# A four-stage kernel (attention, experts, RWKV mixing, experts): fillings over x, an earlier start of the expert stages, batch 6 placed by itself, row tables on GpSimd

## The chip, the cores and the metric

One core of one Trainium2 chip runs the whole program in one launch. The metric is the device time of one execution in microseconds. Engines are TensorE (PE), VectorE (DVE), ScalarE (ACT), GpSimd (POOL) and SyncE (SP, which only issues DMAs here).

## What is computed

x has 8 batches of 512 tokens with 256 channels, all fp32. Four blocks follow each other, each added to x:

```
x = x + attention(layernorm(x))      # linear attention, rope, 3-tap convolution
x = x + experts(layernorm(x))        # 8 experts, top 2 per token, SwiGLU, width 512
x = x + rwkv(x)                      # time mixing (scan over tokens), channel mixing
x = x + experts(layernorm(x))        # same gate and weights
```

The expert block scores 4096 tokens with a gate, takes the best two experts of each, sorts the 8192 pairs by expert and sends each group through its expert's three matrices.

## The kernel before, in words

**Stages.** `phase_attention`, `phase_experts` ("first_"), `phase_mix` (tiles "b_") and `phase_experts` ("second_") run one behind the other, each a block of five hand-written engine programs that wait for each other by semaphores. Between two blocks all engines meet; behind the attention there are two such meetings, one of them after its semaphores are cleared.

**Attention** goes over the batches with two tile sets. ACT normalises, PE transposes (`transposes`, L1066), ACT and DVE write the transposed rows as a high and a low fp32r half (`evacuate_next`, `low_part`), and PE forms every product out of three of such halves (L164 to L166). Beside it the expert matrices are loaded, split and stored: seven experts in the periods (`high_part`, `weight_low`), the eighth as an extra piece in the periods 0, 5 and 6 (`load_extra` and `store_extra` on SP, `high_extra` on ACT, `low_extra` L940 on DVE). In a period DVE runs `low_extra` ahead of the quotient `a_u` and of `a_v` (L1025), and PE's next projections into bank q2 wait for `a_v`. PE's first projection also waits for the semaphore `loaded` (the DMAs of the gate and of `vectors`, the last that SP issues behind the whole of x).

**Routing.** Each token pair needs its row in the sorted table. DVE makes one-hot tables per group of four tiles (one batch): `hot_blocks` (L320, 128x960) and `hot_rows` (L330, 128x1024). ACT scales the first by the token number (`send_tokens`, L349), PE adds up eight products per group in one bank (`place_tokens`, L440), and `order_tokens` (L450) sorts the result. Six groups are early; batches 6 and 7 are late and are ranked together (`late_choices`, `count_choices`, `late_places`, `late_hots`, `final_places`), once the last batch's top experts are known. In the attention the lane numbers that DVE compares with lie in PSUM, in mixing in SBUF.

**Handover.** DVE copies the first row numbers to `gather_token`, and POOL issues three gathers (`first_gathers`, L421) ahead of the end of the stage. In `phase_experts` PE issues 16 fillings (`keep_busy`, L194: products into a bank that nobody reads), waits for the tables that DVE makes of the block bounds (L1356 to L1370, `table_ready`), and only then transposes the first 128 gathered rows (`transpose_x`, L1424). DVE evacuates them (L1377, L1379) behind its tables. After that 71 blocks run, pipelined over two tile sets.

**Mixing.** The head is the serial part: statistics of batch 0, ACT `norm(0)` (L1629), transposes (L2139), `evacuate_xn`, `mix_time`, products k, v, r (`project`, L2158), the scans (L1962, L2006, L2008), `den`, its reciprocal (L2013), `gT` (L2016), `time_product` (L2146). POOL forms `num` for batch 0 in six instructions and then `fk_lo`, the low half of the first channel matrix (L1883); ACT makes `fk_hi` (L1777) behind `carry(0)`, after all weights are in. PE fills with `const.ones` as both operands (128 columns, 44 and 16 of them) and with `fk_hi` (512 columns, 16). Periods follow, in which batch b's channel mixing runs beside batch b+1's time mixing. `finish(b-1, 1)` (L2050) frees the fourth bank of `key_products` (L2233). POOL's `add_channel` adds the result to x.

```
def keep_busy(nc, out, stationary, moving, times):
    for _ in range(times):
        nc.tensor.matmul(out, stationary, moving, start=True, stop=True)
```

Of the kernel before, what the change touches and what calls it, by code (L numbers as in the profile page):

```python
# [44 lines left out]
class Constants:  # L45
# [6 lines left out]
    keep_late: object  # L52
    ones: object
# [170 lines left out]
class Route:  # L224


    def __init__(self, hots, ranks, small, rounded, row_hot, block_hot, sent, bank, placed, sem):
        self.hot = Shelf(hots).take([P, TOPK, EX, T])
        s = Shelf(rounded)
        self.both_early, self.both_late = s.take([P, EX, TE]), s.take([P, EX, TL])  # L230
# [4 lines left out]
        self.earlier_late, self.rank_late, self.chosen_late = s.take([P, EX, TL]), s.take([P, EX, TL]), s.take([P, TOPK, EX, TL])  # L235
# [10 lines left out]
        cells, late = EX * TE, EX * TL  # L246
        self.before, self.all = early_bank[:, 0:cells], early_bank[:, cells:2 * cells]
        self.before_late, self.all_late = late_bank[:, 0:late], late_bank[:, late:2 * late]
# [4 lines left out]
        self.block_hot_ready, self.row_hot_ready = sem("r_block_hot_ready"), sem("r_row_hot_ready")  # L253
        self.sent_ready, self.sent_used = sem("r_sent_ready"), sem("r_sent_used")
# [3 lines left out]
def early_choices(nc, own, r, idx, const):  # L258
# [4 lines left out]
    nc.vector.memset(r.earlier_late[:, 0:1, 0:1], 0.0)  # L263
# [35 lines left out]
def positions(nc, own, r, tiles):  # L299
    own.link(nc.vector.tensor_copy(r.posi[:, :, tiles], r.posf[:, :, tiles]))  # L300
    nc.vector.tensor_scalar(r.lane_at[:, :, tiles], r.posi[:, :, tiles], P - 1, None, ALU.bitwise_and)
    own.link(nc.vector.tensor_scalar(r.block_at[:, :, tiles], r.posi[:, :, tiles], 7, None, ALU.arith_shift_right))

# [20 lines left out]

def hot_rows(nc, dve, r, lane, n):
    depth = len(r.row_hot)
# [7 lines left out]
def late_hots(nc, dve, r, lane):  # L334
    for n in range(EARLY, GROUPS):
        hot_blocks(nc, dve, r, lane, n)
    for n in range(EARLY, GROUPS):
        hot_rows(nc, dve, r, lane, n)
# [20 lines left out]
def late_choices(nc, own, r, idx, const):  # L359
    shape = [P, TOPK, EX, TL]  # L360
    hot = r.hot[:, :, :, TE:T]
    own.link(nc.vector.tensor_tensor(hot, idx[:, :, TE:T].unsqueeze(2).to_broadcast(shape),
                                     const.expert_id[:, :, TE:T].unsqueeze(1).to_broadcast(shape), ALU.is_equal))
    nc.vector.tensor_tensor(r.both_late, hot[:, 0, :, :], hot[:, 1, :, :], ALU.add).then_inc(r.both_ready, 1)


def late_places(nc, dve, own, r, const):


    dve.wait_ge(r.count_done, 2)  # L370
    cells = r.earlier_late.rearrange("p e t -> p (e t)")
    own.link(nc.vector.tensor_tensor_scan(cells[:, 1:EX * TL], r.all_late[:, 0:EX * TL - 1], const.keep_late[:, 1:EX * TL], 0.0,
                                          ALU.add, ALU.mult))
    own.link(nc.vector.tensor_tensor(r.rank_late, r.earlier_late, r.before_late.rearrange("p (e t) -> p e t", t=TL), ALU.add))
    own.link(nc.vector.tensor_tensor(r.rank_late, r.rank_late, r.offset.unsqueeze(2).to_broadcast([P, EX, TL]), ALU.add))
    own.link(nc.vector.tensor_tensor(r.chosen_late, r.hot[:, :, :, TE:T],
                                     r.rank_late.unsqueeze(1).to_broadcast([P, TOPK, EX, TL]), ALU.mult))
    own.link(nc.vector.tensor_reduce(r.posf[:, :, TE:T], r.chosen_late.rearrange("p k e t -> p k t e"), AXX, ALU.add))
    positions(nc, own, r, slice(TE, T))


def final_places(nc, own, r, const):
# [3 lines left out]
    own.link(nc.vector.tensor_tensor(r.total, r.total, r.earlier_late[:, :, TL - 1], ALU.add))  # L386
# [125 lines left out]
def phase_attention(nc, x_dram, qk_w, qk_b, lepe_w, lepe_b, gate_s, cos_t, sin_t,  # L512
# [11 lines left out]
    with ExitStack() as ctx:  # L524
# [101 lines left out]
        def _(sp):  # L626
# [51 lines left out]
            def period(b, par):  # L678
# [4 lines left out]
                if extra is not None:  # L683
                    load_extra(extra)
# [1725 lines left out]
```

## Time and profile before

| what | value |
|---|---|
| three timed runs | 1454.38, 1456.74, 1461.3 us (median 1456.74) |
| the profiled execution | 1451.42 us, of which the span is 1449.7 us |
| TensorE clock granted over the span | 0.963 of full |
| busy: PE, DVE, ACT, POOL | 1354.3, 911.1, 679.4, 622.0 us |
| stages, by the first instruction behind each meeting | attention 0 to 261, experts to 625, mixing to 1087, experts to 1449.7 |

Times in the rows are microseconds from the start of the span. A line of a timeline gives start, length, engine, line of the kernel, operation, output<-inputs, shape and count, and in brackets the idle time of the engine ahead of it with what ended it. The two records of one fp32 product count as two.

### The profile page before, as it was taken

The page shows a single profiled execution, that of the slowest core. Times are in us where ns is not written, and L with a number is a line of the kernel's source. Part 1 is how long each engine was busy: PE and PEld are TensorE (multiplying, and loading weights), DVE is VectorE, ACT ScalarE, POOL GpSimd, SP SyncE. Part 2 cuts the span into 40 slices and gives each one's busy share as a digit, 9 for nine tenths or more (in the row PEclk, how much of TensorE's full clock was granted, in tenths as well). Part 3 has the DMA queues.
Part 4 walks back from the last instruction along what each step waited for, and adds up shares of the span by engine and source line. Part 5 has one row for each costly group of instructions (what it writes and reads, how often), then busy time and mean ns, then how long its engine had stood idle before and what let it go on. Part 6 is the DMA issues. An engine that isn't in the chain of part 4 may idle for free. (4 is left out here: it accounts for less than half of the span.)

```text
span 1449.7 us, 28130 instructions
## 1 busy us (share of the span) xinstructions
PE 1354.3 (93%) x7726; PEld 1149.3 (79%) x7727; DVE 911.1 (63%) x2163; ACT 679.4 (47%) x1525; POOL 622.0 (43%) x567
## 2 busy tenths in 40 slices
PE   6999997799999999965899999999979999999997
PEld 6889896688888888853677787777767888888886
DVE  5877888344444545438878988888754444454543
ACT  3576765133333333324766688666642333333332
POOL 3768660355555555423222222222113555555554
PEclk9999997899999999968999999999989999999999
DMA  7575853566665333360000000000316766643332
GB/s 240 207 273 204 293 202 132 153 166 161 166 159 111 55 55 54 46 217 0 1 15 1 30 29 29 15 15 30 117 45 187 162 167 161 166 86 53 52 58 41
DMA packets 100874, 157.86 MB, mean 109 GB/s; under 512 B 10256, under 2 KB 60688, under 8 KB 100816
## 3 DMA queue, kind: packets, MB, share of 16 engines
q1 hardware_dynamic: 73120, 118.67, 24.1%
q0 software_dynamic: 27264, 37.82, 16.4%
q10 hardware_dynamic: 432, 0.66, 0.2%
q8 instruction: 29, 0.48, 0.1%
q14 instruction: 29, 0.24, 0.1%
HBM read 95.89 MB, written 61.21 MB: 108 GB/s over the span
## 5 line engine op out<-in xcount | busy, mean ns | idle before, releaser
L1293 POOL DMA_INDIRECT out_x<-second_y,second_add_token x71 | 112.6, 1586 | 152.4 <-DMA out_x<-second_y,second_add_token 69.4
L1293 POOL DMA_INDIRECT x_rows<-first_y,first_add_token x71 | 112.8, 1589 | 152.0 <-ACT first_y L1322 95.1
L1284 POOL DMA_INDIRECT xs<-normed_rows,gather_token x136 | 135.2, 994 | 51.2 <-issue 40.7
L1391 DVE TENSOR_TENSOR first_hT_lo<-bank,first_hT_hi 128x512 fp32r<-128x512 f32 x71 | 49.1, 692 | 159.7 <-ACT first_hT_hi L1314 159.7
L1391 DVE TENSOR_TENSOR second_hT_lo<-bank,second_hT_hi 128x512 fp32r<-128x512 f32 x71 | 49.1, 692 | 158.8 <-ACT second_hT_hi L1314 158.8
L164 PE MATMUL bank<-ring,first_xT_hi 128*128 x284 | 118.4, 417 | 2.1 <-DVE first_xT_lo L1379 2.1
L164 PE MATMUL bank<-ring,second_xT_hi 128*128 x284 | 118.3, 417 | 2.1 <-DVE second_xT_lo L1379 2.1
L166 PE MATMUL bank<-ring,first_xT_lo 128*128 x284 | 112.4, 396 | 0.0
L166 PE MATMUL bank<-ring,second_xT_lo 128*128 x284 | 112.4, 396 | 0.0
L165 PE MATMUL bank<-ring,second_xT_hi 128*128 x284 | 111.9, 394 | 0.0
L165 PE MATMUL bank<-ring,first_xT_hi 128*128 x284 | 111.9, 394 | 0.0
L2146 PE MATMUL bank<-b_fv,b_hT 128*128 128x256 f32 x480 | 107.0, 381 | 0.0
L2146 PEld LDWEIGHTS bank<-b_fv,b_hT 128*128 128x128 f32 x480 | 91.3, 192 | 12.2
L1321 ACT ACTIVATE first_add_token<-row_token 128x1 uint32 (+1 forms) x71 | 14.4, 203 | 176.2 <-DMA x_rows<-first_y,first_add_token 145.3
L1321 ACT ACTIVATE second_add_token<-row_token 128x1 uint32 (+1 forms) x71 | 14.4, 203 | 176.0 <-DMA out_x<-second_y,second_add_token 92.3
L1869 POOL TENSOR_TENSOR x<-x,b_fs 128x512 f32<-128x512 f32 (+1 forms) x16 | 25.3, 1581 | 156.3 <-DVE b_fs L2050 156.3
L1455 PE MATMUL bank<-ring,second_hT_hi 128*128 x284 | 75.9, 301 | 0.8 <-ACT second_hT_hi L1314 0.8
L1455 PE MATMUL bank<-ring,first_hT_hi 128*128 x284 | 75.9, 301 | 0.8 <-ACT first_hT_hi L1314 0.8
L1340 ACT ACTIVATE second_g<-bank 128x512 f32<-128x512 f32 x71 | 42.5, 598 | 64.0 <-PE bank L166 64.0
L1340 ACT ACTIVATE first_g<-bank 128x512 f32<-128x512 f32 x71 | 42.5, 598 | 63.9 <-PE bank L166 63.9
L1456 PE MATMUL bank<-ring,second_hT_hi 128*128 x284 | 69.9, 279 | 0.0
L1456 PE MATMUL bank<-ring,first_hT_hi 128*128 x284 | 69.9, 279 | 0.0
(432 smaller groups left out, 3941.2 us busy)
## 6 DMA issues: line engine op xcount, KB each, us to landing
ring<-split_weights SPq DMA_DIRECT2D x192, 256.0 KB, 3.1
a_wraw<-in_L_ffn_w SPq DMA_DIRECT2D x21, 512.0 KB, 6.8
split_weights<-a_whi SPq DMA_DIRECT2D x21, 512.0 KB, 2.7
split_weights<-a_wlo SPq DMA_DIRECT2D x21, 512.0 KB, 3.6
normed_rows<-xg SPq DMA_DIRECT2D x16, 528.0 KB, 3.2
x_rows<-x SPq DMA_DIRECT2D x8, 512.0 KB, 7.6
x<-x_rows SPq DMA_DIRECT2D x8, 512.0 KB, 7.6
out_x<-x SPq DMA_DIRECT2D x8, 512.0 KB, 2.8
```

Source lines behind the costliest of these rows:

```text
L164: nc.tensor.matmul(out, hi, other_hi, start=start, stop=False)
L165: nc.tensor.matmul(out, hi, other_lo, start=False, stop=False)
L166: return nc.tensor.matmul(out, lo, other_hi, start=False, stop=stop)
L1284: nc.gpsimd.indirect_dma_start(xs[q][:], None, normed_dram[:], bass.IndirectOffsetOnAxis(ap=gather_token[q][:], axis=0)).then_inc(loaded[q ...
L1293: nc.gpsimd.indirect_dma_start(x_dram[:], bass.IndirectOffsetOnAxis(ap=add_token[q][:], axis=0), y[q], None, compute_op=ALU.add).then_inc( ...
L1321: nc.scalar.activation(add_token[q][:], column(row_token, i), ACT.Copy)
L1340: nc.scalar.activation(g[par][:], a_bank[par][:], ACT.Silu).then_inc(silu_done, 1)
L1391: nc.vector.tensor_tensor(hT_lo[par][:].rearrange("p k t -> p (k t)"), th_bank[par][:], hT_hi[par][:].rearrange("p k t -> p (k t)").bitcas ...
L1455: nc.tensor.matmul(y_bank[:, 0:C], hT_hi[par][:, k, :], w_hi[:, k * C:(k + 1) * C], start=(k == 0), stop=False)
L1456: nc.tensor.matmul(y_bank[:, 0:C], hT_hi[par][:, k, :], w_lo[:, k * C:(k + 1) * C], start=False, stop=False)
L1869: nc.gpsimd.tensor_tensor(xt, xt, fs[:, h, :].rearrange("p (t c) -> p t c", c=C), ALU.add).then_inc(x3_ready, 1)
L2146: last = nc.tensor.matmul(out[:, j * C:(j + 1) * C], src(i, j), w[:, i, :], start=(i == 0), stop=(i == chunks - 1))
```

## The change

Nine edits, here in the order of the program:

1. Attention, first piece of the eighth expert: loaded ahead of x's last 24 tiles and of the gate and `vectors`, split on ACT and DVE ahead of the loop, stored in period 0. The other two pieces: `low_extra` goes to the end of DVE's period.
2. Fillings at the start of attention and of mixing: `ident` times two tiles of x (512 columns of fp32), 3 for 36 and 4 and 2 for 44 and 16, and they wait for x and the constants, not for the statistics. POOL's `add_bias(0)` waits for the first transposes, since the fillings read x.
3. Row tables: POOL makes those of the groups 1, 3, 5 and 6 in the attention and of group 7 in mixing, in eight instructions of 128x128 each (`pool_rows`); DVE makes a float copy of the lanes for them (`lanef`).
4. One gather ahead of the end of the stage instead of three; the other two stand first in POOL's expert program, ahead of two iotas.
5. Expert stages: 5 fillings for 16; the first rows are transposed, and the first weights given, ahead of `table_ready`.
6. Mixing, head: the first channel matrix is loaded ahead of x's batches 2 to 7, `fk_hi` is made ahead of the evacuation of k, and `fk_lo` by DVE between `mix_time_key(1)` and `decayed_value(0)`.
7. Mixing, periods: `finish(b-1, 1)` ahead of `decayed_value(b+1)`.
8. Mixing, tail: DVE adds the last half batch to x itself and takes half of its statistics earlier; batch 6 is ranked and placed before the last batch's gate products; only batch 7 is left behind them. The fillings ahead of the gate transposes are 14 for 12.
9. One more constant (`keep_last`) on POOL.

```diff
 (attention, SP)
+            load_extra(0)
             sp.dma_start(x[:, 2 * TB:, :], xv[:, 2 * TB:, :]).then_inc(x_in, 16)
 (attention, DVE)
+            low_extra(0)
             def period(b, par):
...
-                if extra_piece(b) is not None:
-                    low_extra(extra_piece(b))
...
+                if extra_piece(b):
+                    low_extra(extra_piece(b))
                 own.pad()
 (attention, PE)
-            pe.wait_ge(var_ready, 1)
-            keep_busy(nc, q2[:, 0:P], const.ones[:], const.ones[:], 36)
+            pe.wait_ge(made, 23)
+            pe.wait_ge(x0_in, 16)
+            keep_busy(nc, q2[:], ident[:], x[:, 0:2, :].rearrange("p t c -> p (t c)"), 3)
 (both stages, POOL)
+def pool_rows(nc, pool, r, const, n):
+    depth = len(r.row_hot)
+    pool.wait_ge(r.lanes_ready, 1 + sum(lo <= n * CH for lo, hi in r.late))
+    if n >= depth:
+        pool.wait_ge(r.sent_used, n - depth + 1)
+    for k in range(TOPK):
+        for j in range(CH):
+            t = n * CH + j
+            last = nc.gpsimd.tensor_scalar(r.row_hot[n % depth][:, k, j, :], const.lane[:], r.lanef[:, k, t:t + 1], None, ALU.is_equal)
+    last.then_inc(r.pool_rows_ready, 1)
 (experts, POOL)
+            for i in range(1, NX - 1):
+                gather(i, i)
             nc.gpsimd.iota(floor[:], ...
 (experts, PE)
-            keep_busy(nc, y_bank[:], const.ones[:], ring[:, 0, 0, 0:H], 16)
+            keep_busy(nc, y_bank[:], const.ones[:], ring[:, 0, 0, 0:H], 5)
+            transpose_x(0, 0)
             pe.wait_ge(table_ready, 1)
             pe.reg_load(slot_reg[0], slot_at[0:1, 0:1])
-            transpose_x(0, 0)
 (mixing, SP, ACT, POOL, DVE)
+            load_weight(fk_raw, f_w_key, fk_in)
             for b in range(2, B):
...
             act.wait_ge(prep, 5)
+            act.wait_ge(fk_in, 16)
+            nc.scalar.activation(fk_hi[:], fk_raw, ACT.Copy).then_inc(fk_hi_ready, 1)
             evacuate_k(0)
...
-            pool.wait_ge(fk_hi_ready, 1)
-            nc.gpsimd.tensor_tensor(fk_lo[:], fk_raw, fk_hi[:].bitcast(F32), ALU.subtract).then_inc(fk_lo_ready, 1)
...
             mix_time_key(1)
+            dve.wait_ge(fk_hi_ready, 1)
+            nc.vector.tensor_tensor(fk_lo[:], fk_raw, fk_hi[:].bitcast(F32), ALU.subtract).then_inc(fk_lo_ready, 1)
             decayed_value(0)
 (mixing, PE)
-            pe.wait_ge(var_ready, 1)
-            keep_busy(nc, xb_[0][:, 0:P], const.ones[:], const.ones[:], 44)
+            pe.wait_ge(x_in[0], 16)
+            with_rows(4)
...
-            keep_busy(nc, xb_[0][:, 0:P], const.ones[:], const.ones[:], 16)
+            with_rows(2)
             project_k(0)
...
             pe.wait_ge(fs_ready, 2 * B)
+            count_choices(nc, pe, route, const, 1)
             pe.wait_ge(varg_ready, B)
-            keep_busy(nc, xb_[4][:], fk_hi[:, 0, 0:P], fk_hi[:, 0, 0:N], 12)
+            keep_busy(nc, xb_[4][:], fk_hi[:, 0, 0:P], fk_hi[:, 0, 0:N], 14)
             gate_transposes(B - 1)
             keep_busy(nc, xb_[4][:], fk_hi[:, 0, 0:P], fk_hi[:, 0, 0:N], 4)
             gate_products(B - 1)
-            count_choices(nc, pe, route, const, 1)
+            place_tokens(nc, pe, route, EARLY)
+            count_choices(nc, pe, route, const, 2)
             keep_busy(nc, xb_[4][:], fk_hi[:, 0, 0:P], fk_hi[:, 0, 0:N], 12)
-            for n in range(EARLY, GROUPS):
-                place_tokens(nc, pe, route, n)
+            place_tokens(nc, pe, route, GROUPS - 1)
             keep_busy(nc, xb_[4][:], fk_hi[:, 0, 0:P], fk_hi[:, 0, 0:N], 2)
             order_tokens(nc, pe, route)
```

## Rows read from the trace of the kernel before

**Rows 1.** Windows: stretch, its length, busy time and count of PE, PEld, DVE, ACT, POOL, then PEclk, DMA share, GB/s.

```profile
635.00:640.00 5.00, 5.00 (x25) 5.00 (x25) 0.00 (x0) 0.00 (x0) 2.53 (x5) 0.50 1.09 386
...
760.00:810.00 50.00, 50.00 (x228) 38.80 (x227) 44.68 (x79) 38.22 (x76) 12.44 (x17) 1.00 0.06 22
```

**Rows 2.** Timeline of PE at the head of mixing.

```profile
629.35 9.65 PE L194 MATMUL bank<-ones 128*128 128x128 f32 x44 [12.52 <-DVE b_mv L1913]
638.80 1.93 PE L2139 MATMUL bank<-ident,b_xn 128*128 128x128 f32 x8
...
645.74 5.30 PE L2158 MATMUL bank<-b_xk,b_wk 128*128 128x512 f32 x8
...
651.75 3.60 PE L2158 MATMUL bank<-b_xv,b_wv 128*128 128x512 f32 x8
...
668.99 5.76 PE L194 MATMUL bank<-b_fk_hi 128*128 128x512 f32 x16 [10.21 <-ACT b_fk_hi L1777]
679.98 5.29 PE L2146 MATMUL bank<-b_wo,b_gT 128*128 128x256 f32 x16 [5.23 <-DVE b_gT L2016]
```

**Rows 3.** Timelines of DVE, ACT and POOL at the head of mixing.

```profile
627.36 1.41 DVE L1910 BATCH_NORM_STATS2 b_bn<-x 128x6 f32<-128x256 f32 x4 [2.03 <-DMA x<-x_rows]
...
659.48 1.23 DVE L1975 TENSOR_TENSOR b_dv<-b_d,b_v 128x1024 f32<-128x1024 f32 x1 [2.51 <-ACT b_d L1709]
...
666.73 6.55 DVE L2013 RECIPROCAL b_den<-b_den 128x1024 f32<-128x1024 f32 x1 [0.16 <-DVE b_den L2011]
673.32 6.61 DVE L2016 TENSOR_TENSOR b_gT<-b_num,b_den 128x512 f32<-128x512 f32 x2
...
632.68 2.07 ACT L1629 ACTIVATE b_xn<-x,b_shifts,b_scales 128x256 f32<-128x256 f32 x4 [6.11 <-POOL b_shifts L1855]
...
666.84 1.90 ACT L1777 ACTIVATE b_fk_hi<-b_hT 128x2048 fp32r<-128x2048 f32 x1
...
674.44 4.94 POOL L1883 TENSOR_TENSOR b_fk_lo<-b_hT,b_fk_hi 128x2048 fp32r<-128x2048 f32 x1
```

**Rows 4.** Timeline of PE at the first handover, from the last placing on.

```profile
250.60 1.71 PE L440 MATMUL bank<-a_qk_hi,a_lepe_hi 128*120 128x128 f32 x8
...
261.45 6.38 PE L194 MATMUL bank<-ring,ones 128*128 128x512 f32 x16 [6.53 <-PEq L1180]
...
269.12 0.50 PE L164 MATMUL bank<-ring,first_xT_hi 128*128 x1 [1.07 <-DVE first_xT_lo L1379]
```

**Rows 5.** Timelines of POOL and DVE at the first handover.

```profile
230.88 0.20 POOL L830 TENSOR_TENSOR a_shift<-a_mv 128x4 f32<-128x4 f32 x1
...
259.49 0.95 POOL L421 DMA_INDIRECT xs<-normed_rows,gather_token  x1 [0.30 <-issue]
...
265.24 0.18 DVE L1370 TENSOR_TENSOR first_pace<-end,first_paced 1x36 int32<-1x36 f32 x1
```

**Rows 6.** Timeline of PE in the attention: its first projection, and one behind `a_v`.

```profile
21.69 0.76 PE L164 MATMUL bank<-a_xnT,a_qk_hi 128*128 128x512 f32 x1 [4.96 <-DMA vectors<-in_vectors]
...
201.12 0.50 PE L164 MATMUL bank<-a_xnT,a_qk_hi 128*128 128x512 f32 x1 [0.80 <-DVE a_v L1025]
```

**Rows 7.** Waits of PE in mixing's periods: total us, times, longest.

```profile
PE bank L2233 <- DVE b_fs L2050: 0.6, 3, 0.2
```

**Rows 8.** Timeline of PE at the tail of mixing and the second handover.

```profile
1067.68 1.09 PE L2139 MATMUL bank<-ident,xg 128*128 128x128 f32 x8 [0.46 <-ACT xg L1629]
...
1080.83 2.49 PE L440 MATMUL bank<-b_over 128*120 128x128 f32 x16 [0.97 <-DVE b_over L330]
...
1087.36 6.43 PE L194 MATMUL bank<-ring,ones 128*128 128x512 f32 x16 [2.83 <-PEq L1501]
...
1095.08 0.50 PE L164 MATMUL bank<-ring,second_xT_hi 128*128 x1 [1.07 <-DVE second_xT_lo L1379]
```

**Rows 9.** Groups of POOL by form: count, busy us, mean ns of one, idle before.

```profile
L829 POOL TENSOR_TENSOR a_mv<-a_mv,neg_half 128x4 f32<-128x4 f32 x16 | 16.6, 1039 | 1.3
...
L497 POOL TENSOR_SCALAR_AFFINE_SELECT block_mask<-block_mask 128x128 f32<-128x128 f32 x1 | 0.3, 315 | 0.0
```

More of the change, by code:

```diff
@@ L52 @@
     keep_late: object
+    keep_last: object
     ones: object
@@ L234, in __init__ @@
         s = Shelf(small)
-        self.earlier_late, self.rank_late, self.chosen_late = s.take([P, EX, TL]), s.take([P, EX, TL]), s.take([P, TOPK, EX, TL])
+        self.earlier_late, self.rank_late = ([s.take([P, EX, hi - lo]) for lo, hi in late] for _ in range(2))
+        self.chosen_late = [s.take([P, TOPK, EX, hi - lo]) for lo, hi in late]
+        self.lanef = s.take([P, TOPK, T])
         self.posf, self.posi = s.take([P, TOPK, T]), s.take([P, TOPK, T], I32)
@@ new lines, in late_places @@
+def late_places(nc, dve, own, r, const, n):
+    dve.wait_ge(r.count_done, 2 + n)
+    lo, hi = r.late[n]
+    tiles = hi - lo
+    keep = const.keep_late if tiles == TL else const.keep_last
+    earlier, rank, chosen = r.earlier_late[n], r.rank_late[n], r.chosen_late[n]
+    cells = earlier.rearrange("p e t -> p (e t)")
+    own.link(nc.vector.tensor_tensor_scan(cells[:, 1:EX * tiles], r.all_late[n][:, 0:EX * tiles - 1], keep[:, 1:EX * tiles], 0.0,
+                                          ALU.add, ALU.mult))
+    own.link(nc.vector.tensor_tensor(rank, earlier, r.before_late[n].rearrange("p (e t) -> p e t", t=tiles), ALU.add))
+    own.link(nc.vector.tensor_tensor(rank, rank, r.offset.unsqueeze(2).to_broadcast([P, EX, tiles]), ALU.add))
+    own.link(nc.vector.tensor_tensor(chosen, r.hot[:, :, :, lo:hi], rank.unsqueeze(1).to_broadcast([P, TOPK, EX, tiles]), ALU.mult))
+    own.link(nc.vector.tensor_reduce(r.posf[:, :, lo:hi], chosen.rearrange("p k e t -> p k t e"), AXX, ALU.add))
+    positions(nc, own, r, slice(lo, hi))
@@ L434, in place_tokens @@
 def place_tokens(nc, pe, r, n):
-    pe.wait_ge(r.row_hot_ready, n + 1)
+    if n in r.by_pool:
+        pe.wait_ge(r.pool_rows_ready, sum(g <= n for g in r.by_pool))
+    else:
+        pe.wait_ge(r.row_hot_ready, sum(g not in r.by_pool for g in range(n + 1)))
     pe.wait_ge(r.sent_ready, n + 1)
@@ L690, in period @@
                     store_piece(b, 2)
-                if extra is not None:
-                    store_extra(extra)
                 if not is_first(b):
@@ L1827, in _ @@
             row_finish(B - 1)
-            for n in range(EARLY, GROUPS):
-                send_tokens(nc, act, route, const, n)
+            send_tokens(nc, act, route, const, GROUPS - 1)
             region_rows(nc, act, route)
```

185 lines of the change are left out of this document (111 added, 74 removed).

## The prediction

> **What bounds the kernel now.** I read the page first, then windows over whole stages, then PE's timeline and waits, and at each place where PE stands still the timelines of the others. Inside the mixing periods PE is busy 50.00 of 50 us at the full clock [rows 1], and the expert stages and the attention read the same way, so the other engines' time there is free. The time that a change can take without removing products lies where PE idles or fills: the head of mixing, the two handovers into the expert stages, the start of attention. The head of mixing is the largest. PE's first transposes start at 638.80, though the rows they read are ready at 632.68 + 2.07 = 634.75; the 44 fillings, 9.65 us long, stand in between [rows 2, 3]. Those fillings keep PE busy all the time and the clock stays at 0.50, 1.2 GHz [rows 1]. At the far end of the head the two `gT` instructions take 6.61 us, and `time_product` waits for them until 679.98 [rows 2, 3].
>
> **The head of mixing (edits 2 and 6).** The new fillings start when x is in, about 627.3 [rows 3]. One fp32 product of 512 columns costs what a pair of records costs in the projections: 3.60 / 4 = 0.9 us in the group of v, at the full clock, 5.30 / 4 = 1.3 in that of k, partly at the half [rows 2]; wholly at 1.2 GHz it is twice 0.85, an estimate of 1.7. Four end between 632.5 and 634.1, ahead of 634.75. So the transposes start 638.80 - 634.8 = 4.0 us earlier. A clock that has risen by then brings them from 1.93 to 1.09 us, 0.8 less [rows 2, 8]. The products of k at the full clock cost 3.6 and not 5.30: 1.7. Together 6.5. That the 16 narrow fillings ahead of k become two wide ones (1.8 us) may give some tenths more, up to 1 us; I leave it to the range. `fk_hi` (1.90 on ACT [rows 3]) now stands ahead of k's evacuation: behind `norm(1)`, which by this schedule ends some 1.6 us before the first half of k, so it costs about 0.3; what is queued behind it is k, then v, then the relus for `d`. Should its load come late (it is ahead of 3 MB of x, at the 386 GB/s of [rows 1] 1 MB lasts 2.7 us, in by 636), it would cost all of its wait; I see none.
>
> `fk_lo` costs DVE about 2.2 us (2048 columns at the rate of 1024 in 1.23), and DVE idles 2.51 us at exactly that place, ahead of `dv`, for ACT [rows 3]; that idle time is its cover, and without it up to 2.2 us are paid. What it leaves behind is worth more. `gT` is two instructions of 128x512 with two SBUF inputs, some 0.65 us each by the same rate, and took 6.61: from 674.44 to 679.38 POOL runs `fk_lo`, and DVE's second product ends at 679.93, half a microsecond after it [rows 3]. The Trainium skill (GPSIMD Engine Reference, "Key points") says that GpSimd shares its SBUF interfaces with VectorE, with contention for instructions with two SBUF inputs; the trace agrees, with 6.61 us for what would be 1.3. Without it the second product follows POOL's last `num` at 674.44 and ends near 675.2, 4.7 us earlier. Sum so far 6.5 - 0.3 + 4.7 = 10.9. `time_product` ran at the half clock after a gap of 5.23 us (5.29 us [rows 2]); the gap becomes about 2.5 us, the clock should hold, 1.7 less. That makes **-12.6**. Ends: -9 (only the 4.0 and 4.7, clock low throughout) and -14.
>
> **Handovers (edits 4 and 5).** At the first one PE's program begins 1.0 us after POOL's third gather ends, 259.49 + 0.95 against 261.45 [rows 4, 5]. Two gathers fewer, 0.95 + 0.30 each, move the meeting by 2.5. Behind it the first product waited for 16 fillings (6.38), transposes and 1.07 of evacuation: 269.12 - 261.45 = 7.67. Now DVE's tables bind, they end 265.42 - 261.45 = 4.0 after the meeting, plus 1.1 for the evacuation queued behind them on DVE: 5.1, so 2.6 less [rows 4, 5]. POOL's two moved gathers stand ahead of the iotas that the tables need at their end; 2.5 us plus two short ones is under the 3.8 us between the meeting and DVE's last table [rows 4, 5]. Against it goes the clock. Five fillings are over after 2.1 us, then PE nearly idles for 3 us. The first block has 12 products of 512 columns, 0.43 us at 1.2 GHz and 0.21 at 2.4: at most 2.6 lost, I take 2.0. First handover -2.5 - 2.6 + 2.0 = **-3.1** (ends -5.1 and 0). At the second one PE began 1087.36 and its product at 1095.08, 7.7 again [rows 8]; same 2.6 and 2.0, and no gain of the meeting, since mixing ends with one meeting that need not wait for queued gathers: **-0.6** (ends -4 and +2).
>
> The fillings that are cut are where a page speaks against the change. The trace: the 16 fillings of 261.45 ran 0.40 us each, nearly all at 1.2 GHz, and the product behind them was at 2.4 GHz [rows 4]. The Trainium skill (TensorE: Matmul & The Clock Gate, "What's actually happening") says that the half clock is the default and that only sustained activity releases it. By it five fillings buy nothing and the first blocks pay; the first rival below works that out.
>
> **Start of attention (edits 1 and 2).** PE's first projection waits 4.96 us for `vectors`, the last of the DMAs it needs, until 21.69 [rows 6]; the earlier transposes gain nothing here. The 512 KB of the extra piece now go ahead: at 386 GB/s [rows 1] 1.4 us later. The first products run at the half clock in any case. Part of the 1.4 is lost from slow products only: **+1.0** (ends 0 and +2). Moving `low_extra` (1024 columns, so about 1.2 us on DVE by the rate of [rows 3]) behind `a_v` removes a wait of 0.80 us [rows 6], one of three such, in the periods 0, 5 and 6; in its new place DVE waits for POOL's additions to x anyway, and that wait covers it. **-2.2** (ends -2.4 and 0). `keep_last`, `add_bias` behind the transposes: nothing, PE's wait for `vectors` covers them.
>
> **Row tables and batch 6 (edits 3 and 8).** A POOL instruction of 128x128 with one input is between 0.315 us (an affine select) and 1.04 us (the power of 128x4) [rows 9]; the select has the same size and one input, so 0.35 to 0.4. In the attention POOL is free from 231.08 [rows 5] and has 32 of them until PE places group 6 at 250.60 [rows 4]. PE gets there behind its own six fillings, so DVE's saved tables end up as DVE idle time; group 6's eight start when its lanes are known; between that and PE's start DVE fitted three tables of about 1.2 us each, and eight of 0.35 to 0.4 are 3.2. **0** (ends -0.5 and +2). In mixing the add on DVE and the early statistics bring the last normalised rows forward by about a us, but PE, behind placing that is not earlier, filled 12 times until 0.46 us ahead of the gate transposes at 1067.68 [rows 8], and two more fillings take 0.5: the transposes stand where they did. Behind the last gate only 8 of the 16 placing products of 2.49 us are left [rows 8]: -1.25; half-size tables and final places earlier: -0.3. POOL's table 7 and DVE's small two-input instructions meet there. **-1.3** (ends -3 and +2).
>
> **Periods (edit 7).** `b_fs` ends PE waits of 0.2 us, three shown, one to be expected in each of six periods [rows 7]: **-1.0** (ends -2 and 0).
>
> **Sum.** -12.6 - 3.1 - 0.6 + 1.0 - 2.2 - 1.3 - 1.0 = -19.8. The profiled execution's 1451.42 us become 1431.6. That execution lies 5.3 us under the median of the three timed runs; for a median I subtract from 1456.74 and say **1437**.
>
> **Rivals.** *The clock stays low (0.20).* Both expert stages' first two blocks at 1.2 GHz cost 5.1 instead of 2.0 each, and the head of mixing only gives its 9: the sum is -19.8 + 6.2 + 3.6 = -10, 1447. For it: narrow fillings that kept PE full never raised the clock [rows 1]. Against: wide ones did, at every place where they ran [rows 2, 4]. *The stall moves (0.07).* `fk_hi` and `fk_lo` are not covered, 1.9 + 2.2, and `gT` still meets POOL's `num`: the head gives 7, the sum is -14 with other terms lower near -9, 1448. *More than forecast (0.06).* Five fillings are enough and the meeting of the second handover moves: -25 to -28, 1430. *GpSimd is the bound (slower, 0.04).* The four row tables of attention are a chain of 32 instructions. At c us each they fit before 250.60 up to (250.6 - 231.1) / 32 = 0.6 us. Each further 0.1 costs 3.2 us there and 0.8 in mixing; the other terms' 19.8 us are used up at c = 1.1, and 0.5% is lost from 1.3. For it: 1.04 us exist [rows 9]; against: that is a power, and the select of equal size is 0.315. *No effect to speak of (0.03)*: the edits only shift waits.
>
> **How the numbers follow.** The forecast has 0.60. About 0.5%, 7.3 us, is what a measurement of this kernel can tell from no change. Faster by more than that: forecast 0.60, nearly all of the clock's 0.20, more than half of the stall's, the larger gain: 0.90. Same 0.06, slower 0.04. The range runs from the larger gain taken from the profiled time (1425) to the low clock's 1447.
>
> **What would show it.** Right: PE's first transposes in mixing 7.5 us behind x's landing (now 11.4) and about 1.0 us long; `gT` under 3 us; `time_product` about 40 us behind x's landing (now 52.6); the first expert product 5 us after the meeting; no PE wait on `a_v`. Wrong: POOL `row_hot` instructions over 0.6 us each, PE placing that waits for POOL, PEclk 0.5 over more than 6 us behind each handover, or a head of mixing that ends less than 9 us earlier.

## The result and the profile after

| | before | after |
|---|---|---|
| timed runs, median | 1458.11 us (4 runs, 1454.38 to 1461.30) | 1442.47 us (4 runs, 1437.56 to 1444.31) |
| the profiled execution | 1451.42 us, span 1449.7 | 1444.31 us, span 1442.1 |
| granted clock over the span | 0.963 | 0.957 |
| busy: PE, DVE, ACT, POOL | 1354.3, 911.1, 679.4, 622.0 us | 1344.4, 908.2, 679.0, 645.1 us |

The ratio of after to before is 0.9888 with a 95% interval of 0.9859 to 0.9916: 15.6 us faster between the medians, where 19.7 were forecast. The two profiled executions differ by only 7.1. Where that comes from is part of the finding, so here are both traces as a ladder of landmarks on PE. A step is what the stretch since the landmark above lost (+) or gained (-). A counting product belongs to `count_choices`, a placing product to `place_tokens`, the table of the order is the last product of `order_tokens`, and the meeting is read at PE's first filling behind it. "Rows of x landed" is read on DVE before and after.

| landmark | before | after | step |
|---|---|---|---|
| first projection of the attention | 21.69 | 24.12 | +2.4 |
| first counting product (last period) | 204.03 | 201.52 | -4.9 |
| first placing product | 225.61 | 229.41 | +6.3 |
| table of the order | 254.67 | 259.50 | +1.0 |
| expert program begins (the meeting) | 261.45 | 263.78 | -2.5 |
| first product of block 2 | 273.48 | 276.63 | +0.8 |
| rows of x landed, mixing | 627.36 | 630.38 | -0.1 |
| second product of k | 685.11 | 675.57 | -12.6 |
| gate of batch 6 | 1045.57 | 1035.98 | -0.1 |
| table of the order | 1084.13 | 1075.82 | +1.3 |
| the meeting | 1087.36 | 1077.91 | -1.1 |
| first product of block 2 | 1099.43 | 1091.61 | +1.6 |
| end of the span | 1449.7 | 1442.1 | +0.2 |

One stage, the head of mixing, carries the gain: -12.6 between the landing of x and the second product of k. All other steps together are a loss of 5.0 in this pair of traces. Timeline of PE at the head of mixing in the changed kernel, beside [rows 2]:

```profile
630.39 5.11 PE L195 MATMUL bank<-x,ident 128*128 128x512 f32 x8 [10.51 <-DMA x<-x_rows]
637.92 1.06 PE L2218 MATMUL bank<-ident,b_xn 128*128 128x128 f32 x8 [2.42 <-ACT b_xn L1688]
640.52 3.45 PE L195 MATMUL bank<-x,ident 128*128 128x512 f32 x4 [1.54 <-ACT b_xnT L1720]
643.80 3.60 PE L2237 MATMUL bank<-b_xk,b_wk 128*128 128x512 f32 x8
...
663.13 5.90 PE L195 MATMUL bank<-b_fk_hi 128*128 128x512 f32 x16 [7.98 <-DVEq L2070]
672.01 3.72 PE L2225 MATMUL bank<-b_wo,b_gT 128*128 128x256 f32 x16 [2.98 <-DVE b_gT L2074]
675.57 3.60 PE L2237 MATMUL bank<-b_xk,b_wk 128*128 128x512 f32 x8
```

The transposes stand 7.5 us behind x's landing (11.4 before) and are 1.06 long; k runs in 3.60 and not 5.30; the output product follows 41.6 us behind the landing (52.6 before) and takes 3.72 where it took 5.29. On DVE, beside [rows 3], the stall of `gT` is gone and `fk_lo` has found its gap:

```profile
653.24 2.28 DVE L2130 TENSOR_TENSOR b_fk_lo<-b_hT,b_fk_hi 128x2048 fp32r<-128x2048 f32 x1
655.84 1.22 DVE L2033 TENSOR_TENSOR b_dv<-b_d,b_v 128x1024 f32<-128x1024 f32 x1 [0.31 <-ACT b_d L1768]
...
669.67 2.29 DVE L2074 TENSOR_TENSOR b_gT<-b_num,b_den 128x512 f32<-128x512 f32 x2
```

The idle time ahead of `dv` fell from 2.51 to 0.31 us: that idle time was the cover that the prediction named. The first handover, PE beside [rows 4], then DVE and POOL beside [rows 5]:

```profile
256.46 1.06 PE L483 MATMUL bank<-a_qk_hi,a_lepe_hi 128*120 128x128 f32 x8 [1.44 <-POOL a_qk_hi L344]
...
263.78 2.47 PE L195 MATMUL bank<-ring,ones 128*128 128x512 f32 x5 [4.02 <-PEq L1236]
266.05 0.63 PE L1482 MATMUL bank<-ident,xs 128*128 128x128 f32 x2
270.14 0.79 PE L165 MATMUL bank<-ring,first_xT_hi 128*128 x1 [3.46 <-DVE first_xT_lo L1437]
...
276.63 0.50 PE L165 MATMUL bank<-ring,first_xT_hi 128*128 x1 [1.08 <-DVE first_xT_lo L1437]
```

```profile
268.52 0.17 DVE L1424 TENSOR_TENSOR first_paced<-end,first_behind 1x24 f32<-1x24 f32 x1 [1.48 <-POOL first_behind L1351]
```

```profile
251.76 4.65 POOL L344 TENSOR_SCALAR a_qk_hi<-lane,a_qk_raw 128x128 fp32r<-128x128 f32 x8 [1.12 <-DVE a_qk_raw L311]
...
264.35 1.55 POOL L1335 DMA_INDIRECT xs<-normed_rows,gather_token  x1 [1.60 <-POOLq L1236]
266.20 1.67 POOL L1335 DMA_INDIRECT xs<-normed_rows,gather_token  x1 [0.30 <-issue]
267.89 0.29 POOL L1349 IOTA first_floor<- 1x48 f32 x1
268.15 0.26 POOL L1351 IOTA first_behind<- 1x48 f32 x1
```

Three things were not forecast: PE's last placing waits for POOL's table, DVE's last table waits 1.48 us for an iota that stands behind the two moved gathers, and the first block's products are 0.79 and 0.63 long, against 0.50 and 0.40 in block 2. At the tail of mixing and behind the second meeting PE beside [rows 8], then POOL's table at that tail:

```profile
1065.41 5.20 PE L195 MATMUL bank<-b_fk_hi 128*128 128x512 f32 x12
1073.37 1.69 PE L483 MATMUL bank<-b_over 128*120 128x128 f32 x8 [2.76 <-POOL b_over L344]
...
1075.82 0.26 PE L493 MATMUL bank<-b_over 120*128 120x72 f32 x1
...
1082.86 0.69 PE L1482 MATMUL bank<-ident,xs 128*128 128x128 f32 x2 [2.48 <-DMA xs<-normed_rows,gather_token]
1084.62 0.79 PE L165 MATMUL bank<-ring,second_xT_hi 128*128 x1 [1.07 <-DVE second_xT_lo L1437]
```

```profile
1067.81 5.50 POOL L344 TENSOR_SCALAR b_over<-lane,b_al 128x128 fp32r<-128x128 f32 x8 [13.38 <-DVE b_al L311]
```

Eight instructions in 5.50 us are 0.69 each, in the attention (4.65) 0.58. Behind the second meeting there is a fourth thing that was not forecast: the five fillings end after 2.47 us, and PE's transposes then wait 2.48 us for the first gathered rows to land. Before, the 16 fillings (6.43 [rows 8]) covered that landing. And the first projection, beside [rows 6]:

```profile
24.12 0.77 PE L165 MATMUL bank<-a_xnT,a_qk_hi 128*128 128x512 f32 x1 [10.69 <-DMA vectors<-in_vectors]
```

### The profile page after: what moved, and what is told of

Its sections match the earlier page's. It is cut to its first block and busy times, and to the rows that moved or that the text cites. A ratio compares the mean times of both kernels' runs of the same rounds, so it can differ in the third digit from the quotient of the medians.

```text
span 1442.1 us, 27994 instructions
## 1 busy us (share of the span) xinstructions
PE 1344.4 (93%) x7630; PEld 1134.9 (79%) x7631; DVE 908.2 (63%) x2179; ACT 679.0 (47%) x1525; POOL 645.1 (45%) x607
## 3 DMA queue, kind: packets, MB, share of 16 engines
q0 software_dynamic: 27264, 37.82, 16.5%
## 5 line engine op out<-in xcount | busy, mean ns | idle before, releaser
L1335 POOL DMA_INDIRECT xs<-normed_rows,gather_token x140 | 140.4, 1003 | 46.2 <-issue 41.5
L2225 PEld LDWEIGHTS bank<-b_fv,b_hT 128*128 128x128 f32 x480 | 91.7, 192 | 12.4
L1929 POOL TENSOR_TENSOR x<-x,b_fs 128x512 f32 (+1 forms) x15 | 24.4, 1629 | 141.7 <-DVE b_fs L2108 141.7
```

What stands on the lines that cost most here:

```text
L1335: nc.gpsimd.indirect_dma_start(xs[q][:], None, normed_dram[:], bass.IndirectOffsetOnAxis(ap=gather_token[q][:], axis=0)).then_inc(loaded[q ...
L2225: last = nc.tensor.matmul(out[:, j * C:(j + 1) * C], src(i, j), w[:, i, :], start=(i == 0), stop=(i == chunks - 1))
```

## The experiments

Each set of runs has its own runs of the kernel before beside it, and the sets were taken on different chips. So medians are compared inside a set, and sets with each other by their ratios to the kernel before.

### Is the head of mixing the whole gain?

The kernel before, with these edits alone:

```
-            keep_busy(nc, xb_[0][:, 0:P], const.ones[:], const.ones[:], 44)
+            pe.wait_ge(x_in[0], 16)
+            with_rows(4)
...
+            load_weight(fk_raw, f_w_key, fk_in)
...
+            nc.scalar.activation(fk_hi[:], fk_raw, ACT.Copy).then_inc(fk_hi_ready, 1)
             evacuate_k(0)
...
+            nc.vector.tensor_tensor(fk_lo[:], fk_raw, fk_hi[:].bitcast(F32), ALU.subtract).then_inc(fk_lo_ready, 1)
             decayed_value(0)
```

> The kernel before with the edits of the head of mixing alone (wide fillings over x, the load and the split of fk_hi early, fk_lo on VectorE). My theory: the head holds nearly all of the gain, so this kernel is 12.5 us faster than before, about 1444 to 1446, and from the landing of x to the second product of k it takes 45 us where before took 57.8; the two gT take about 2.3 us. Rival (the gain comes as much from the handovers and the attention as from the head): 5 to 8 us faster.

Measured: 1442.07 us against 1456.38, ratio 0.9905 (0.9885 to 0.9924). The changed kernel in its own two sets stands at 0.9888 and 0.9899 (below). So the head gives 14.3 us between medians (11 to 17 by the interval), and all the other edits together give nothing that these runs can tell from zero. Landing of x to the second product of k took 46.4 us here (630.77 to 677.15): 1.2 more than in the changed kernel, since the output product ran at the lower clock, 5.41 us.

### Who makes the row tables?

```
-                      (l1, q1, q0), placed, ((TE, T),), (1, 3, 5, 6), lambda name: sem("a_" + name))
+                      (l1, q1, q0), placed, ((TE, T),), (), lambda name: sem("a_" + name))
...
-                      (xb_[5], xb_[5], xb_[0]), placed, ((TE, T - CH), (T - CH, T)), (GROUPS - 1,), sem)
+                      (xb_[5], xb_[5], xb_[0]), placed, ((TE, T - CH), (T - CH, T)), (), sem)
...
-            pool_rows(nc, pool, route, const, GROUPS - 1)
```

> The changed kernel with every row table back on VectorE, GpSimd makes none. My theory: GpSimd's tables of 8 instructions at 0.58 to 0.69 us end last at both places, PE waits 1.4 us for them in the attention and 2.8 in the tail of mixing; without them the tail of mixing is 2.5 to 2.8 us shorter (from the last transposes of the gate to the table of the order 17.7 becomes about 15), the attention 0 to 1.4, sum 3 to 4 us faster than the changed kernel. Rival (VectorE had no room, that is why tables were shared): VectorE's 1.2 us for each table move the last tables by 1.2 in mixing and up to 4.8 in the attention, and the kernel is 2 to 4 us slower than the changed one.

Measured: 1433.82, ratio 0.9858 (0.9832 to 0.9884). Its interval overlaps that of the changed kernel's first set (0.9859 to 0.9916) and just touches that of the second (0.9883 to 0.9916), so the times alone leave the gain open. The trace shows the mechanism. PE at the tail of mixing:

```profile
1061.83 5.16 PE L195 MATMUL bank<-b_fk_hi 128*128 128x512 f32 x12
1067.03 1.03 PE L483 MATMUL bank<-b_over 128*120 128x128 f32 x8
...
1068.55 0.27 PE L493 MATMUL bank<-b_over 120*128 120x72 f32 x1
```

No wait is left there: from the gate's last transposes to the table of the order it takes 14.1 us (1054.44 to 1068.55) against 17.7 in the changed kernel and 16.5 before. In the attention, from the fillings behind the last statistics to the table of the order, 25.2 us against 26.6 (25.6 before). So GpSimd's tables cost 3.5 us in mixing and 1.4 in the attention. The rival, that DVE has no room, is out: DVE makes the last table of mixing in 1.22 us. With the tables on DVE, the tail of mixing is 2.4 us shorter than before, so without edit 3 the tail's edits do more than the 1.3 that were forecast.

### Fillings: shape and count

The head of mixing with the narrow form, starting at the same moment and as long in sum:

```
-                keep_busy(nc, xb_[0][:], ident[:], x[:, 0:2, :].rearrange("p t c -> p (t c)"), times)
+                keep_busy(nc, xb_[0][:, 0:P], const.ones[:], const.ones[:], times)
-            with_rows(4)
+            with_rows(24)
...
-            with_rows(2)
+            with_rows(16)
```

> The changed kernel with the fillings of the head of mixing in the narrow form again (24 and 16 products of 128 columns in the place of 4 and 2 pairs of 512), starting at the landing of x, of the same length in sum. My theory: the shape decides whether the clock rises; with narrow ones the transposes take 1.9 us and the first products of k 5.3, and the head is 2.5 us longer than in the changed kernel. Rival (only when the fillings start and end matters): the head is as long as in the changed kernel, transposes 1.05, k 3.6.

Measured: 1445.67, ratio 0.9928 (0.9900 to 0.9956). The head took 48.8 us (631.34 to 680.17) and not 45.2. PE, and the window of [rows 1] (columns as there):

```profile
631.34 5.38 PE L195 MATMUL bank<-ones 128*128 128x128 f32 x24 [11.00 <-DMA x<-x_rows]
638.86 1.94 PE L2218 MATMUL bank<-ident,b_xn 128*128 128x128 f32 x8 [2.14 <-ACT b_xn L1688]
642.34 3.68 PE L195 MATMUL bank<-ones 128*128 128x128 f32 x16 [1.54 <-ACT b_xnT L1720]
645.81 6.18 PE L2237 MATMUL bank<-b_xk,b_wk 128*128 128x512 f32 x8
```

```profile
635.00:640.00 5.00, 2.86 (x15) 2.71 (x15) 2.09 (x11) 2.08 (x4) 2.02 (x6) 0.50 1.06 381
```

The same window in the changed kernel:

```profile
635.00:640.00 5.00, 1.57 (x10) 0.86 (x8) 2.09 (x11) 3.05 (x6) 2.01 (x7) 1.00 1.06 369
```

The clock is 2.4 GHz there after 5.11 us of wide fillings, and 1.2 after 5.38 of narrow ones. The kind of filling decides here, not when it starts or how long it lasts, and it is worth 3.6 us (2.5 expected: k took 6.18, not 5.3). It isn't chance of one execution: all eleven profiles with wide fillings in the head have k in 3.6 to 3.7 us, and the two with narrow ones have 5.30 and 6.18. The experiment changed more than the width: the wide fillings are fp32 products of `ident` and x, the narrow ones fp32r products of `const.ones` with itself. What speaks for the width is that the 16 fillings of the expert stages are fp32r too, with `const.ones` as one operand, but 512 columns wide, and the block behind them is at 2.4 GHz after 6.38 us [rows 4], while behind 44 narrow ones, 9.65 us long, the transposes still took 1.93 [rows 2]. The same width was not tried in both types at one place. The start of the attention repeats the result: the transposes took 1.93 us behind 36 narrow fillings (7.06 to 15.00, before; the same in `head_alone`) and 1.09 behind three wide ones (5.98 to 11.44, changed kernel; the same in ten of eleven profiles, 1.97 in `fk_lo_on_pool`).

The expert stages with 16 fillings again:

```
-            keep_busy(nc, y_bank[:], const.ones[:], ring[:, 0, 0, 0:H], 5)
+            keep_busy(nc, y_bank[:], const.ones[:], ring[:, 0, 0, 0:H], 16)
```

> The changed kernel with 16 fillings at the start of both expert stages again. My theory: the first block runs at the full clock, but waits for the fillings as before did; meeting to the first product of block 2 is 12.0 (first stage) and 12.1 (second) as in before, where the changed kernel has 12.9 and 13.7, so the kernel is 1 to 2.5 us faster than the changed one. Rival (my forecast: the shorter wait is worth more than the clock): 1 to 2 us slower than the changed kernel.

Measured: 1440.65, ratio 0.9907 (0.9877 to 0.9937), which settles nothing. The trace says more. Meeting to block 2:

```profile
262.28 6.14 PE L195 MATMUL bank<-ring,ones 128*128 128x512 f32 x16 [4.03 <-PEq L1236]
...
269.71 0.49 PE L165 MATMUL bank<-ring,first_xT_hi 128*128 x1 [1.08 <-DVE first_xT_lo L1437]
...
274.06 0.50 PE L165 MATMUL bank<-ring,first_xT_hi 128*128 x1 [1.07 <-DVE first_xT_lo L1437]
```

11.8 us, against 12.9 with five fillings; in the second stage 12.3 against 13.7. The block starts later behind the meeting (7.4 against 6.4) and is through sooner, for its products are at the full clock. My forecast had it the other way. In the seven profiles with five fillings and nothing else changed at the handovers, block 2 comes 12.1 to 13.1 us behind the first meeting and 13.6 to 14.0 behind the second, so the gain of 16 fillings is clear in the second stage and 0.3 to 1.3 us in the first.

### The stall of gT

`fk_lo` back on GpSimd behind `num`, in the changed kernel:

```
-            nc.vector.tensor_tensor(fk_lo[:], fk_raw, fk_hi[:].bitcast(F32), ALU.subtract).then_inc(fk_lo_ready, 1)
...
+            nc.gpsimd.tensor_tensor(fk_lo[:], fk_raw, fk_hi[:].bitcast(F32), ALU.subtract).then_inc(fk_lo_ready, 1)
```

> The changed kernel with fk_lo back on GpSimd, behind its num products, where before had it. My theory: the 6.6 us of the two gT came from GpSimd's fk_lo beside them; here they take 6 us or more again where the changed kernel has 2.3, and the head of mixing, landing of x to second product of k, is 3.7 to 4.3 us longer than its 45.2 (in time_product's start). Rival (gT was long because of its inputs or of the reciprocal before it): gT stays at 2.3 us and the head at 45.

Measured: 1444.24, ratio 0.9937 (0.9920 to 0.9954). The timelines of DVE, POOL and PE:

```profile
669.86 6.60 DVE L2076 TENSOR_TENSOR b_gT<-b_num,b_den 128x512 f32<-128x512 f32 x2
```

```profile
670.97 4.95 POOL L1943 TENSOR_TENSOR b_fk_lo<-b_hT,b_fk_hi 128x2048 fp32r<-128x2048 f32 x1
```

```profile
676.51 6.13 PE L2225 MATMUL bank<-b_wo,b_gT 128*128 128x256 f32 x16 [7.24 <-DVE b_gT L2076]
```

6.60 us against 2.29 with the same inputs behind the same reciprocal: the instruction beside them on GpSimd makes the difference. The interval lies clear of both sets of the changed kernel. The cost is larger than expected, 52.1 us for the head (630.41 to 682.48) against 45.2: behind the stall of 4.3 us PE's gap is 7.24 and its product runs in 6.13, another 2.4.

### The handover

```
-            for i in range(1, NX - 1):
-                gather(i, i)
             nc.gpsimd.iota(floor[:], pattern=[[PIECES, EX], [1, PIECES]], base=2 - 2 * PIECES, channel_multiplier=0,
...
+            for i in range(1, NX - 1):
+                gather(i, i)
...
             transpose_x(0, 0)
+            keep_busy(nc, y_bank[:], const.ones[:], ring[:, 0, 0, 0:H], 4)
```

> The changed kernel with GpSimd's two iotas ahead of its two gathers in the expert stages, and four more fillings between the transposes and the first product. My theory: VectorE's wait of 1.5 us for the iota goes, so the first product is 4.9 us behind the meeting in place of 6.4 to 6.7, and PE, busy nearly all the time, is at the full clock by the first block or in it: meeting to block 2 is 10 to 10.5 us, sum of both stages 5 us faster than the changed kernel. Rival (the clock stays low in the first block whatever PE does in these 3 us): only the 1.5 us each, 3 us faster.

Measured: 1439.93, ratio 0.9900 (0.9875 to 0.9924). Meeting to block 2 took 9.3 us (269.92 to 279.20) in the first stage and 11.8 in the second, 3.6 and 1.9 less than in the changed kernel. PE in the first stage:

```profile
272.47 1.32 PE L195 MATMUL bank<-ring,ones 128*128 128x512 f32 x4
274.84 0.49 PE L165 MATMUL bank<-ring,first_xT_hi 128*128 x1 [1.05 <-DVE first_xT_lo L1437]
```

The wait for the iota is gone and the first block is at the full clock. In the second stage PE still waited 1.59 us for the first gathered rows, the four fillings behind it ran at the lower clock (2.05 us), and with them six of the first block's twelve products. So the clock part of my theory held in one stage only, and not even there in every execution: in `all_four_moves` below, with the same instructions, the four fillings of the first stage took 2.06 us and block 2 came 9.8 us behind the meeting. The median shows little of the 5.5 us; in this profile the attention's table came late, at 265.63.

### The start of the attention

The two small loads ahead of the second load of x:

```
+            sp.dma_start(gate_s[:], gate).then_inc(loaded, 16)
+            sp.dma_start(vectors_s[:], vectors).then_inc(loaded, 16)
             sp.dma_start(x[:, TB:2 * TB, :], xv[:, TB:2 * TB, :]).then_inc(x1_in, 16)
...
-            sp.dma_start(gate_s[:], gate).then_inc(loaded, 16)
-            sp.dma_start(vectors_s[:], vectors).then_inc(loaded, 16)
```

> The changed kernel with the loads of gate and vectors issued ahead of all but the first load of x. My theory: PE's first projection waits for these two small loads alone, since the normalised rows are split by 15.95; it starts at about 16.5 in place of 24.1, and the kernel is 4 to 7 us faster than the changed one, less than 7.6 because batch 1 may then wait for other loads. Rival (the weights of the expert pieces or the rest of x come next and bind): PE's wait moves into the first period, and 0 to 2 us are left.

Measured: 1439.26, ratio 0.9896 (0.9877 to 0.9916): no different from the changed kernel. The rival was right. PE, then ACT:

```profile
15.79 0.54 PE L165 MATMUL bank<-a_xnT,a_qk_hi 128*128 128x512 f32 x1 [2.67 <-DVE a_xnT L946]
36.66 1.97 PE L1186 MATMUL bank<-ident,a_kr 128*128 128x128 f32 x8 [6.40 <-DVE a_kr L1038]
```

```profile
22.27 2.08 ACT L800 ACTIVATE a_xn<-x,a_shift,a_mv 128x256 f32<-128x256 f32 x4 [5.71 <-POOL a_shift L879]
24.25 0.67 ACT L827 ACTIVATE a_ex<-bank,a_qk_bias 128x512 f32<-128x512 f32 x1
```

The 8.3 us won at the first projection were gone at the second, which starts at 50.19 (48.93 in the changed kernel): 6.40 of them went into a wait for `kr`, since the exponentials of batch 0 are queued on ACT behind the normalisation of batch 1. Behind that wait the transposes take 1.97 us, where the changed kernel has 1.04. So the queue was turned as well, in the first period alone:

```
-                if not is_last(b):
+                if not is_last(b) and not is_first(b):
                     normalise(xn[1 - par], mv, shift, b + 1, xn_ready)
...
+                if is_first(b):
+                    normalise(xn[1 - par], mv, shift, b + 1, xn_ready)
```

> The changed kernel with the loads of gate and vectors early, and in the first period of the attention the exponentials of batch 0 ahead of the normalisation of batch 1 on ScalarE. With the loads alone PE's first projection moved from 24.1 to 15.8, but PE then waited 6.4 us for kr, because ScalarE's first exponential stood behind that normalisation until 24.2. My theory: the exponentials begin at 17 to 18, kr ends near 30 and not 36.6, PE does not wait over 2 us for it and keeps its clock; the second projection starts 6 to 7 us ahead of the changed kernel's 48.9, and the kernel is 5 to 8 us faster than the changed one. Rival (the loads of the expert weights or GpSimd's bias addition bind next): 2 to 3 us faster, as with the loads alone.

Measured: 1431.21 against 1452.20, ratio 0.9854 (0.9838 to 0.9871), 21 us under the kernel before and, by the ratios, 5 to 7 us under the changed kernel, as the theory had it. PE:

```profile
16.05 0.47 PE L165 MATMUL bank<-a_xnT,a_qk_hi 128*128 128x512 f32 x1 [2.66 <-DVE a_xnT L949]
40.11 0.50 PE L165 MATMUL bank<-a_xnT,a_qk_hi 128*128 128x512 f32 x1 [1.06 <-DVE a_xnT L949]
```

PE has no wait over a microsecond between these two, and the second projection stands at 40.1 where the changed kernel has 48.9.

### The change again, and the moves together

> The changed kernel without an edit, on the same chip as the two that follow. Theory: in identical code the reduced clock falls in other places from one execution to the next (in five profiles with the same attention its last table came at 258.0 to 265.6 us), so medians within 0.4% of the first ones: 1438 to 1447. Rival: the spread belongs to the kernels, and this one repeats to 0.1%.

Measured: 1439.58 (1437.27 to 1440.50) against 1452.87, ratio 0.9899 (0.9883 to 0.9916). Both sets of the changed kernel agree. Its profiled execution, though, has the table of the order at 256.58, with identical code 2.9 us ahead of the first profile.

> The changed kernel with the four moves that helped alone: row tables on VectorE, early loads of gate and vectors with the first exponentials ahead of the normalisation, iotas ahead of the gathers, four more fillings ahead of the first expert product. Theory: they lie at different places and add up: small loads and exponentials 11, row tables 4 to 5, handovers 5 us, together 20 under the changed kernel, about 1422. Rival: what is gained in the attention is lost again in its last period or its tail, which wait for other engines, and half remains, about 1430.

Measured: 1424.66, ratio 0.9790 (0.9766 to 0.9814): 28.2 us under the kernel before, 14.9 under the changed one. PE in it, from the start to the second handover:

```profile
15.58 0.47 PE L165 MATMUL bank<-a_xnT,a_qk_hi 128*128 128x512 f32 x1 [2.67 <-DVE a_xnT L949]
...
245.71 0.96 PE L483 MATMUL bank<-a_qk_hi,a_lepe_hi 128*120 128x128 f32 x8
...
248.79 0.27 PE L493 MATMUL bank<-a_xnT 120*128 120x72 f32 x1 [0.60 <-DVE a_xnT L437]
...
1058.19 1.03 PE L483 MATMUL bank<-b_over 128*120 128x128 f32 x8
...
1074.24 0.50 PE L165 MATMUL bank<-ring,second_xT_hi 128*128 x1 [1.08 <-DVE second_xT_lo L1440]
```

The last placing of either stage waits for nothing. Meeting to block 2 takes 12.4 us in the second stage (1061.82 to 1074.24), 1.3 less than in the changed kernel. The total lies between my 1422 and the rival's 1430. The moves add up to three quarters of the 20 that I had summed.

> As the kernel with the four moves, but 7 fillings ahead of the first transposes of an expert stage and 2 behind them in place of 5 and 4, and 10 in place of 12 ahead of the last placing of mixing, where VectorE's table is ready 0.7 us before the fillings end. Theory: the second stage, where the first gather lands 1.6 us behind the fillings, no longer waits idle and is 0.5 to 1 us shorter, the tail of mixing 0.5 us, together 1 to 1.5 us faster than its neighbour. Rival: the first stage loses as much by later transposes, and there is no difference.

Measured: 1422.24, ratio 0.9782 (0.9764 to 0.9800). The second stage took 11.7 us to block 2 (1058.61 to 1070.26), the tail of mixing 14.1 (1042.40 to 1056.51), as its neighbour. The two can't be told apart by their times, so the 1 to 1.5 us expected stay open.

## Why the prediction was right, and where not

**The head of mixing: right, step by step.** -12.6 forecast, -12.6 in the ladder. Transposes 11.4 to 7.5 behind x's landing (-3.9, forecast 4.0) and 0.87 shorter; k 1.7 shorter; from there to the output product -4.3 (forecast -0.3 + 4.7); that product 1.6 shorter (1.7). The last term isn't safe, and there the forecast had luck: of the eleven profiles that have `fk_lo` on VectorE seven show 3.72 us for that product, behind gaps of 2.98 to 3.30 us, and four show 5.41 to 6.63, behind gaps of 2.15, 2.27, 2.86 and 3.61. Over the ten of them with wide fillings the head took 44.7 to 48 us against 57.8 in the one profile with the old head. `fk_lo_on_pool` showed the stall to be GpSimd's doing, `narrow_in_head` the clock to hang on the kind of filling, and `head_alone` that hardly anything else was gained.

**Handovers: the meeting right, the sum wrong.** The gathers taken out of the way brought the first meeting forward by 2.5, as forecast. The step that failed is "2.6 less" behind it. The first product came 6.4 and 6.7 us behind the meetings and not 5.1, so only 1.3 and 1.0 were saved. In both stages DVE's tables ended late, since the moved gathers (1.55 and 1.67 us each in the first stage, where 0.95 was assumed) stood ahead of the iotas, and DVE waited 1.48 us for them. In the second stage the rows of the first gather also landed only 5 us behind the meeting (1082.86 against 1077.91), a wait for which the sum had no term. The "2.0 lost" to the clock was about right: from the first block's first product to the transposes behind it took 5.0 and 5.3 us, where before had 2.9. With the transposes behind the first block, and in the second stage these at 1.2 GHz too, the forecast of -0.6 for either stage behind the meeting became +0.8 and +1.6. The five fillings bought nothing, and `sixteen_fillings` reached block 2 sooner. The Trainium skill (TensorE: Matmul & The Clock Gate, "What's actually happening") says that only sustained activity releases the half clock, which spoke against this edit; the trace agrees with it, with 0.63 us for a product of the first block behind five fillings and 0.40 behind sixteen. The second meeting did gain 1.1, where I had excluded it.

**Row tables: the price was wrong.** The step "0.35 to 0.4 us", read off an affine select of the same size, [rows 9], measured 0.58 in the attention and 0.69 in mixing. In the attention the last table alone is what binds: POOL stood idle for 1.12 us until its lanes were known, then took 4.65, where the forecast had 3.2 against the 3.6 of DVE's three tables, and PE waited 1.44. The rival's chain of 32 instructions was not the bound, since POOL has idle gaps of 1.82 and 1.12 us inside it; that the measured 0.58 lies near the rival's limit of 0.6 is chance. In mixing, where only one table was left, I had priced no wait at all, and there PE waited 2.76: the tail lost 1.3 in place of winning 1.3. `dve_tables` confirms both. The rival had the right engine, but the bound was one late table and not the chain, and it was too small to turn the sign.

**Attention.** The loads moved ahead cost 2.4 and not 1.0: SP began to issue the load of `vectors` at 17.44, before at 15.68, and it took 0.6 us longer to land. The waits on `a_v` (0.72, 0.77 and 0.80 us) are gone, as forecast, and from the first projection to the counting product 4.9 were gained, more than the 2.2 counted; two more waits of PE for DVE that before had in its second period (0.86 at 71.65 and 0.75 at 74.46) are gone too. Then the last period gave 6.3 back. It has PE waits of 0.62 and 0.97 us for ACT and DVE, and behind them the clock is at half. A window of the changed kernel:

```profile
215.00:220.00 5.00, 5.00 (x25) 5.00 (x24) 1.98 (x8) 2.53 (x12) 0.00 (x0) 0.50 0.01 2
```

The prediction had no step for that. Only part of this loss belongs to the change: from the counting product to the first placing before and `head_alone` have 21.6 us, and the six profiles with the changed attention have 22.7 (`sixteen_fillings`), 24.8 (`change_again`) and four times 27.8 or 27.9. So at least 1.1 us go with the change, and up to 5.2 more with where the clock is at half. Why PE waits there now, and what sets the clock, was not tried.

**Periods.** "-1.0" for the waits on `b_fs` [rows 7]: they are gone, and the stretch between the second product of k and the gate of batch 6 is 0.1 shorter. Removing three waits of 0.2 us moved no end; where they are taken up again I did not trace, so that step of the sum failed and the cause stays open.

**The sum.** The step that failed beyond single terms is that one profiled execution stood for the kernel. That of before (1451.42) was faster than each of its four timed runs, and that of after (1444.31) equal to the slowest of its own, so the profiles differ by 7.1 and the medians by 15.6. The ladder's losses in the attention are partly those of one execution. The edits outside the head were forecast at -7.2 and came to about nothing. So the total of 15.6 came near the forecast through the head alone: its 12.6 is traced, and no trace assigns the other 3.0, which are within what the medians can tell.

## What to carry to other kernels

Look for the stage where PE fills or idles, and there for what the filling is: here a few wide fp32 products, begun when their data is in, raised the clock that 44 narrow fp32r ones did not. Before work is moved to a slower engine, price it with an instruction of the same operation and find what waits for its end at every place, for the short tail bit harder than the long one. When a wait is removed at the start, follow the queue of the next engine at once: the loads alone gave nothing, the loads and the turned queue about 6 us by the ratios.

## What was unexpected in the hardware

Six profiles share the changed kernel's attention, instruction for instruction (the first, `change_again`, and the runs with narrow fillings, `fk_lo`, 16 fillings and the iotas). In them the table of the order came at 259.50, 256.58, 259.72, 259.29, 257.99 and 265.63 us. Two profiles with the attention of before had it at 254.67 and 259.10. With it goes where the granted clock is at half: in the first profile it is between 215 and 220 (the window above), and the products of `kz` and `el` there take 3.42 us, 1.85 in before. An edit worth 3 us in the attention can't be judged from one profile of this kernel.

GpSimd's gathers of one kind took 0.94 to 1.67 us: 1.24, 1.55 and 1.67 for the first three of the first expert stage, 1.13, 0.96 and 1.58 in the second, and 0.95 for the third of before [rows 5]. I had priced the moved ones at 0.95 us. What lengthens them was not tried.
